# A kernel of four attentions and four feed-forward layers: the softmax maximum of the narrow attentions carried in spare rows of the score product

## The reference

```python
q = (layernorm(x) @ Wq).reshape(B, S, 32, 16)
k = (ctx @ Wk).reshape(B, S, 8, 16)          # repeated for 4 query heads each
v = (ctx @ Wv).reshape(B, S, 8, 16)
scores = einsum('bhqd,bhkd->bhqk', q, k) / 4
probs = softmax(scores, axis=-1)
x = x + einsum('bhqk,bhkd->bhqd', probs, v).reshape(B, S, 512) @ Wo
```

## Time and profile before

| | |
|---|---|
| median of 3 runs | 2164.53 us (2162.89 to 2166.49) |
| profiled execution, first to last instruction | 2159.1 us |
| PE busy in it | 1995.0 us, 92% |
| DVE, ACT, POOL busy | 1587.5, 1335.2, 204.8 us |

### The profile page before, as it was taken

The page is one execution under the profiler, slowest core; times in us unless marked ns, Lnnn a source line. Parts: engine busy times, 40 slices in busy tenths (PEclk is TensorE's granted clock), DMA queues, the critical chain, the costliest instruction groups (busy, mean ns, idle before and its releaser), DMA issues.

```text
span 2159.1 us, 39910 instructions
## 1 busy us (share of the span) xinstructions
PE 1995.0 (92%) x13920; PEld 1147.6 (53%) x13920; DVE 1587.5 (74%) x4091; ACT 1335.2 (62%) x3897; POOL 204.8 (9%) x207
## 2 busy tenths in 40 slices
PE   4887999999999999999976797999999999999778
PEld 2554444466666666666643464444555555555444
DVE  6666555677777777777768576767798889988773
ACT  3665212287777777777753565434788888888621
POOL 3674000000000000000000463000000000000020
PEclk8899999999999999999998998999999999999999
DMA  5231111224444544453530331111044333343200
GB/s 215 62 55 16 59 59 40 78 58 95 108 81 91 110 85 91 81 114 74 95 79 20 74 69 36 59 69 49 16 93 92 71 90 93 62 90 83 62 6 39
DMA packets 318935, 157.65 MB, mean 73 GB/s; under 512 B 309648, under 2 KB 309648, under 8 KB 311312
## 3 DMA queue, kind: packets, MB, share of 16 engines
q1 hardware_dynamic: 318736, 155.09, 31.2%
HBM read 77.44 MB, written 2.10 MB: 37 GB/s over the span
## 4 chain that ended last, share of the span: by engine, by line
PE 59%; DVE 26%; ACT 8%; issue 4%; DMA 1%; POOL 1%; SPq 0%; ACTq 0%; DVEq 0%; POOLq 0%
PE bank L702 54%; ACT hid L1628 4%; DVE hid L2221 3%; DVE masked L2180 3%; DVE negmax L2184 2%; DVE wa_lo L1746 2%; DVE x L2193 2%; DVE oT_lo L2211 2%; DVE negmax_n L1920 1%; DVE wo_lo L1746 1%; ACT bd_hi L1505 1%; PE bank L794 1%; PE bank L810 1%; PE bank L811 1%; DVE xnT_lo L1813 1%
## 5 line engine op out<-in xcount | busy, mean ns | idle before, releaser
L702 PE MATMUL bank<-xnT_hi,wa_hi 128*128 128x512 f16 x736 | 279.1, 379 | 4.2 <-PE bank L702 1.8
L702 PE MATMUL bank<-xnT_hi,wa_lo 128*128 128x512 f16 x736 | 279.1, 379 | 0.0
L702 PE MATMUL bank<-xnT_lo,wa_hi 128*128 128x512 f16 x736 | 279.1, 379 | 0.0
L702 PE MATMUL bank<-wo_hi,oT_hi 128*128 128x512 f16 x576 | 221.5, 385 | 28.2 <-DVE oT_lo L2211 27.2
L2221 DVE SCALAR_TENSOR_TENSOR hid<-probs,inv_total,hid 128x256 f16<-128x256 f32 (+1 forms) x512 | 179.9, 413 | 81.4 <-ACT hid L1628 81.4
L702 PE MATMUL bank<-wo_hi,oT_lo 128*128 128x512 f16 x576 | 221.4, 384 | 0.0
L702 PE MATMUL bank<-wo_lo,oT_hi 128*128 128x512 f16 x576 | 221.2, 384 | 0.0
L702 PE MATMUL bank<-wa_hi,xnT_hi 128*128 128x512 f16 (+3 forms) x640 | 203.1, 323 | 6.7 <-DVE hid L1882 2.6
L702 PE MATMUL bank<-wa_lo,xnT_hi 128*128 128x512 f16 (+3 forms) x640 | 203.0, 323 | 0.0
L702 PE MATMUL bank<-wa_hi,xnT_lo 128*128 128x512 f16 (+3 forms) x640 | 202.9, 323 | 0.0
L1587 ACT ACTIVATE probs<-bank,negmax,rms_r 128x256 f32<-128x256 f32 x256 | 140.9, 560 | 96.3 <-DVE negmax L2177 96.3
(11 more groups left out here) (252 smaller groups left out, 4860.3 us busy)
## 6 DMA issues: line engine op xcount, KB each, us to landing
raw<-in_w_qkv_dram SPq DMA_DIRECT2D x18, 1536.0 KB, 7.0
raw<-in_w_out_dram SPq DMA_DIRECT2D x18, 1024.0 KB, 5.3
raw<-in_w_ffn_dram SPq DMA_DIRECT2D x15, 1024.0 KB, 4.9
pT<-hid SPq DMA_TRANSPOSE x256, 3.1
raw<-in_w_ffn0d_dram SPq DMA_DIRECT2D x7, 512.0 KB, 3.5
x<-in_x_dram SPq DMA_DIRECT2D x4, 512.0 KB, 5.5
expert_b<-in_expert_b_dram SPq DMA_DIRECT2D x1, 2048.0 KB, 9.4
kT<-k SPq DMA_TRANSPOSE x128, 2.4
```

Of the source, the lines that this page charges most:

```text
L702: mm = pe.matmul(dst, l, r, start=start and k == 0, stop=stop and k == n - 1)
```

## The change

The negated maximum no longer has a matmul of its own. The keys' fourth slot of 32 rows, which was zero, holds the constant 64, and the fourth slot of the queries holds, for `turned_scores`, the high and low f16 halves of the negated maximum divided by 64. The score product itself then adds it. For `scores` of the same batch, which runs before, the queries' fourth slot is still zero.

- `max_hi` on ACT is now two instructions: the f16 high part of `negmax_n / 64`, and a f32 copy of `negmax_n / 64` (`max_scaled`), from which POOL's `max_lo` subtracts.
- `max_parts` grows from 128 to 512 columns f16, and `turn_max` makes eight transposes in place of one: four column blocks, into bank S0 and once more into bank Q.
- `spread_max` writes rows 96 to 127 of `qst`, heads 0 and 1 by DVE from S0, heads 2 and 3 by ACT from Q, two instructions of 32 x 512 elements each, in place of one DVE instruction of 128 x 512. On ACT it stands in step 7 between `soft` and `v_part`. PE's `turned_scores` of step 0 and the next `scores` wait for both.
- `turned_scores` is one matmul. The constants `chunk_rows`, `max_chunk` and the bf16 identity go; POOL fills the keys' fourth slot with 64 at the start of each narrow attention.
- The slots of `q_parts` and `k_parts` are in another order; their instructions are the same in number and size.

```diff
-        max_rows = bd_flat[:, 2048:3072].bitcast(BF16).rearrange("p (a b) -> p a b", a=2)
+        max_rows = qst[96:128, :, :].rearrange("p a (c h t) -> p a h c t", c=4, h=HPG)
...
-            def ones():
+            def ones(n):
...
-                pool.memset(k_parts[:, :], 0.0).then_inc(nb_kzero, 1)
+                pool.memset(k_parts[:, :], 0.0).then_inc(k_zero, 1)
+                pool.wait_ge(k_zero, n + 1)
+                for m in range(2):
+                    op = pool.memset(k_part_slots[:, 3, m], MAX_SCALE)
+                op.then_inc(nb_kzero, 1)
...
-                pool.tensor_tensor(max_slots[:, 1], negmax_n[:, :].rearrange("p (m h) -> p m h", m=2), max_slots[:, 0],
-                                   ALU.subtract).then_inc(nb_max_lo, 1)
+                src = max_scaled[:, :].rearrange("p (m c h) -> p m c h", m=2, c=4)
+                pool.tensor_tensor(max_slots[:, 1], src, max_slots[:, 0], ALU.subtract).then_inc(nb_max_lo, 1)
...
             pool.tensor_copy(ident_16[:, :], ident)
-            pool.tensor_copy(ident_b[:, :], ident)
-            pool.tensor_copy(chunk_rows[:, :, :], c("max_chunk").unsqueeze(2).broadcast_to([P, G, P]))
...
                         if b:
                             pe.wait_ge(nb_max_rows, BB)
+                            pe.wait_ge(nb_max_rows_act, BB)
...
                 def turn_max(b):
                     pe.wait_ge(nb_max_lo, n * B + b + 1)
-                    pe.transpose(bank[S0][:, :].bitcast(BF16)[:, 0:P], max_parts[:, :], ident_b[:, :]).then_inc(nb_maxT, 1)
+                    if b == 0:
+                        pe.wait_ge(nb_rope_q if n == 0 else nb_qlo, 2)
+                    for to in (S0, Q):
+                        for ch in range(4):
+                            mm = pe.transpose(halves16(to)[:, ch * P:(ch + 1) * P], max_parts[:, ch * P:(ch + 1) * P],
+                                              ident_16[:, :])
+                    mm.then_inc(nb_maxT, 1)
...
                         pe.wait_ge(nb_max_rows, n * B + b + 1)
+                        pe.wait_ge(nb_max_rows_act, n * B + b + 1)
...
-                    to = bank[PT0 + j % 2][:, :]
-                    pe.matmul(to, kst[:, b % 2, ch, m, :], qst[:, b % 2, ch * 512:(ch + 1) * 512], start=True, stop=False)
-                    pe.matmul(to, chunk_rows[:, g, :], max_rows[:, b % 2, :], start=False, stop=True).then_inc(ng_turned, 1)
+                    pe.matmul(bank[PT0 + j % 2][:, :], kst[:, b % 2, ch, m, :], qst[:, b % 2, ch * 512:(ch + 1) * 512],
+                              start=True, stop=True).then_inc(ng_turned, 1)
...
                         act.wait_ge(nb_maxT, BB)
-                    src = negmax_n[:, :].rearrange("p (m h) -> p m h", m=2)
-                    act.activation(max_slots[:, 0], src, ACT.Copy).then_inc(nb_max_hi, 1)
+                        act.wait_ge(nb_max_lo, BB)
+                    src = negmax_n[:, :].rearrange("p (m c h) -> p m c h", m=2, c=4)
+                    act.activation(max_slots[:, 0], src, ACT.Copy, scale=1 / MAX_SCALE)
+                    act.activation(max_scaled[:, :], negmax_n[:, :], ACT.Copy, scale=1 / MAX_SCALE).then_inc(nb_max_hi, 1)
+
+                def spread_max(b):
+                    act.wait_ge(nb_maxT, n * B + b + 1)
+                    src = halves16(Q)[96:128, 0:512].rearrange("p (c t) -> p c t", c=4)
+                    for h in (2, 3):
+                        op = act.activation(max_rows[:, b % 2, h], src, ACT.Copy, scale=c("max_head")[96:128, h:h + 1])
+                    op.then_inc(nb_max_rows_act, 1)
...
                         soft(j)
+                    if g == 7 and f < B:
+                        spread_max(f)
                     if g == 7 and p < B:
                         v_part(p)
                         k_part(p)
...
                     if g == 0 and BB:
-                        dve.wait_ge(nb_max_lo, BB)
+                        dve.wait_ge(nb_max_hi, BB)
...
                     dve.wait_ge(nb_maxT, BB + 1)
-                    if b >= 2:
-                        dve.wait_ge(ng_turned, (BB - 1) * G)
-                    dve.tensor_tensor(max_rows[:, b % 2, :].rearrange("p (h t) -> p h t", h=HPG),
-                                      bank[S0][:, :].bitcast(BF16)[:, 0:P].unsqueeze(1).broadcast_to([P, HPG, P]),
-                                      c("max_head").unsqueeze(2).broadcast_to([P, HPG, P]), ALU.mult).then_inc(nb_max_rows, 1)
+                    src = halves16(S0)[96:128, 0:512].rearrange("p (c t) -> p c t", c=4)
+                    for h in (0, 1):
+                        op = dve.tensor_scalar(max_rows[:, b % 2, h], src, c("max_head")[96:128, h:h + 1], None, ALU.mult)
+                    op.then_inc(nb_max_rows, 1)
```

More of the change, by code:

```diff
@@ L43 @@
 WOUT = HPG * D
+MAX_SCALE = 64.0
 NORM_EPS = 1e-5
@@ L54 @@
 _at = 0
-for _name, _n in (("ident", P), ("max_head", HPG), ("max_chunk", G), ("iota", 16), ("gate_s", FC), ("up_s", FC),
+for _name, _n in (("ident", P), ("max_head", HPG), ("iota", 16), ("gate_s", FC), ("up_s", FC),
                   ("down_s", D), ("q1", 1), ("k1", 1), ("q3", 1), ("k3", 1), ("router1_b", 8),
@@ L293, in build @@
         inv_total_n = sb("inv_total_n", [2, 16], F32)
-        negmax_n = sb("negmax_n", [32], F32)
+        negmax_n, max_scaled = sb("negmax_n", [32], F32), sb("max_scaled", [32], F32)
         hid = sb("hid", [2, D], F32)
         hid_flat = hid[:, :, :].rearrange("p a b -> p (a b)")
[L297 to L301, removed]
+        ident_16 = sb("ident_16", [P], F16)
+        max_parts = sb("max_parts", [4 * P], F16)
+        max_slots = max_parts[:, :].rearrange("p (c s m j h t) -> p s j t m c h", s=4, m=2, j=2, h=HPG, t=2)[:, 3, 0]
         qst = bd_hi
@@ L326, in build @@
         k_parts = squares[:, 0:512].bitcast(F16)
-        q_part_slots = q_parts.rearrange("p (c m s d) -> p s m c d", m=2, s=4, d=ND)
-        k_part_slots = k_parts.rearrange("p (c u s d) -> p s u c d", u=4, s=4, d=ND)[:, :, 0:4:3]
+        q_part_slots = q_parts.rearrange("p (c s m d) -> p s m c d", m=2, s=4, d=ND)
+        k_part_slots = bass.AP(k_parts.tensor, k_parts.offset,
+                               [list(k_parts.ap[0]), [2 * ND, 4], [P + ND, 2], [2 * P, 4], [1, ND]])
         def v_heads(t):
@@ L472, in build @@
                              "nb_max_rows", "nb_inv", "nb_on", "nb_olo", "nb_y", "ng_max"))
+        nb_max_rows_act, k_zero = sem("nb_max_rows_act"), sem("k_zero")
         n_consts, nb_qn, nb_kn, nb_qparts, nb_kparts, ng_plo = (
@@ L671, in _ @@
             pool.tensor_copy(ident_16[:, :], ident)
-            pool.tensor_copy(ident_b[:, :], ident)
-            pool.tensor_copy(chunk_rows[:, :, :], c("max_chunk").unsqueeze(2).broadcast_to([P, G, P]))
             pool.memset(max_parts[:, :], 0.0)
-            ones()
+            ones(0)
             ctx_low(0)
@@ L685, in _ @@
             pool.wait_ge(w_y, UNITS)
-            ones()
+            ones(1)
             zeros(1)
@@ L2533, in lay_out @@
     cols = {
-        "ident": np.eye(P), "max_head": (row % 64 < 32) & (row // 2 % HPG == np.arange(HPG)),
-        "max_chunk": (row % 64 < 32) & (row // 64 * 4 + row % 64 // 8 == np.arange(G)), "iota": np.broadcast_to(np.arange(16), (P, 16)),
+        "ident": np.eye(P), "max_head": (row >= 96) & (row % 16 < 8) & (row // 2 % HPG == np.arange(HPG)), "iota": np.broadcast_to(np.arange(16), (P, 16)),
         "gate_s": a["L0_ffn_gate_s"].reshape(FC, P).T, "up_s": a["L0_ffn_up_s"].reshape(FC, P).T,
```

## The result

The change makes the kernel slower. In five runs of each the median went from 2163.95 us to 2175.7 us (2175.08 to 2181.86); the ratio is 1.0055 [1.0043, 1.0068], some 11.8 us. The forecast of 2164.8 us, no change, with a range up to 2171, was wrong. Of the five runs after, three took 2175.1 to 2175.7 us and two, the profiled one among them, 2180 to 2182 at a lower granted clock (0.966 against 0.968 to 0.970), so the traces of this kernel, e8's too, show some 4 us more than the median lost.

What follows compares the result with a forecast made beforehand. The prediction took PE, DVE and the keys' way to alternate as bound, the keys' DMA setting when scores start. First attention -1.5 us and second +1.8 gave +0.3: 2164.8 us, no change; range 2158.5 to 2171.

Steps and rivals of the forecast that it cites:

- both as a rival: In the narrow attentions, keys' DMA takes over everywhere: issued 0.6 and 1.15 us later, +5.4 us, 2169.9 us; chance 0.12.
- the clock in the weight stretches: While DVE splits weights, PE idles and falls to half clock: two such stretches and longer first wait, +4.8 us; chance 0.10.
- The matmul removed: turned_scores loses its second matmul: 0.65 us at steps 0 to 2, 0.1 at 3 to 5; 0.97 us a batch.
- The transposes: On PE between max_lo and the output projection's second half: seven more at 0.055 us each, 0.39 us a batch.
- The spread: At the hand-over: DVE's pair 0.7 to 1.3 us, ACT's about 1.09; PE's step 0 0.16 to 0.24 us later.
- The keys' DMA: Behind ACT's spread, issued 0.4 and 0.95 us later; with 3.1 us landings, scores start 0.2 and 0.1 us earlier.
- First hand-overs: First two batches of each attention, without output projection as cover: first attention -0.6 us, second +1.4 us.
- PE's busy time: Over the whole kernel, PE's busy time should fall by about 22 us: 28.2 us of matmuls less the added transposes.
- The profiled execution: Profiled span, 2159.1 us, lies 5.4 us under the median; taken as a part outside first and last instruction, unchanged.
- Costed at nothing: ACT's second copy of the maxima ends during POOL's low part; uncovered it would be 0.24 us a batch, 3.8 us.

Runs made afterwards that it cites:

- e8: The changed kernel again, unedited, for a second profiled execution: 2180.55 us (span 2178.8).
- e1: The kernel before without the second matmul of turned_scores alone; the maximum is still found, transposed and spread: 2157.11 us, ratio 0.9965.
- e7: The changed kernel with a second matmul in turned_scores again, one that adds zeros: 2176.66 us, ratio 1.0049 against the kernel before.
- e9: The kernel before again, unedited, for a second profiled execution: 2166.81 us (span 2164.9).
- e5: The kernel before with seven more transposes of the same tile in turn_max, results unused: 2168.64 us, ratio 1.0020.
- e6: The kernel before with ACT's two spread instructions ahead of v_part, results unused, and PE's step 0 waiting for them: 2169.40 us, ratio 1.0026.
- e2: The changed kernel with v_part and k_part ahead of spread_max on ACT: 2170.91 us, ratio 1.0040 against the kernel before.
- e4: The changed kernel with four transposes, DVE alone spreading one column block of all heads at a time, each step awaiting its block: 2158.86 us.

## Why the prediction was wrong

Its mechanism was right in the main. It named the keys' DMA as what sets the scores, ACT's spread as what delays it, and both as a rival; it named the clock in the weight stretches as another. What failed was the sizes: the keys' issue was put too early, PE's clock stood at nothing in the sum, and the two rivals were taken as alternatives. Here both happened, 11.1 us in the attentions where they were given +5.4 and +4.8.

- *The matmul removed.* The 0.1 us for steps 3 to 5 was, if anything, too much: the stretch took 5.81 us before and 5.80 after. Steps 6 and 7 went as said: `max_lo` and the transposes come 0.21 us earlier. The 0.97 us a batch on PE's path is there in e1 where nothing else is late; in the kernel after the time stays when the whole matmul is put back (e7), in part because the clock comes back with it.
- *The transposes.* 0.39 us for seven was measured (0.62 against 0.23). The term of the sum was right and its place wrong: they stand ahead of ACT's spread, so they delay the keys by as much as PE.
- *The spread.* DVE's pair took 0.90 us, within its bounds. ACT's took 1.25, near the upper bound of 1.3; 1.09 was taken, from the exponentials, though the row with a scale for each partition was the nearer one. PE's step 0 is 0.44 us later (2.01 less 1.36, less 0.21), not 0.16 to 0.24.
- *The keys' DMA: the first term that broke the sum.* Against the transposes its issue was put 0.61 and 1.17 us later (0.4 and 0.95 on the clock of the old timeline, plus the 0.22 that the transposes come earlier). Measured were 1.10 and 1.51. Some of the gap is that pair (0.16 and 0.18 us). The rest is `v_part` and `k_part`: in the first attention ACT's `k_part` ends 0.85 us behind the spread where 0.55 was reckoned. The 0.55 came from a stretch in which `v_part` began 0.12 us before the exponential ahead of it had ended, and `k_part` 0.13 us before `v_part` had; now each begins 0.03 us behind the end of the one before. The landing of 3.1 us was right, and so was its reason: the queries' and the keys' DMA are issued 4.0 us apart, 2.7 and 2.3 before. With the measured issue the sum of a steady batch comes out: 1.10 - 0.21 = 0.89 us later on the clock, less the 0.4 that the keys had to spare, is the +0.5 of the first attention; 1.51 - 0.21 = 1.30 less 0.8 to 1.1 is +0.2 to +0.5 in the second, where +0.43 and +0.45 were measured. The prediction had -0.3 and -0.2. It gives the other batches too: with the distances of e9, 4.18 and 4.88 us from the issue to the scores where the landing was long, nothing is lost in the 4th interval of the first attention and 0.3 us won in the 5th of the second (+0.08 and -0.30 measured).
- *First hand-overs.* Predicted -0.6 and +1.4 us, measured +2.7 and +3.0. In the first attention step 0 comes 1.0 us later, as said (2.50 against 1.45 and 2.01 against 1.02), but nothing is won back. In the first of the first attention the scores start hardly later (7.63 us against 7.50, e8 and e9); what came was a fall of the clock in the stretch behind them, 1.25 us for the twelve matmuls; in the second of it a fall took 0.84. The first of the second attention was about right, 1.2 predicted and 1.48 measured. The second of it had 0.2 and took 1.55, of which 1.0 is eighteen matmuls at the half clock.
- *PE's clock: the second term.* The rival's mechanism was right and its places too few: it was priced for two stretches of the second attention and given 0.10, and the sum had nothing for it. The trace after has four falls in places that were full, two of them in the first attention. An estimate of the two terms from these rows: 0.49 and 0.34 us more of issue in five steady batches each are 4.2 us, the four falls 4.3.
- *PE's busy time.* 22 us less was predicted. In the attentions it fell by 7.1 us against e9: matmuls at the half clock count twice. The windows show the lower clock; how much of the missing 15 us is the clock's and how much is that of records of longer matmuls behind a wait is not settled.
- *The profiled execution.* The 5.4 us between the span and the median were taken as a part outside the instructions. Each run's time is only 1.8 us above its span (2180.1 and 2178.3); the rest was one execution that ran faster than the others. It didn't touch the sum.
- *Costed at nothing.* ACT's second copy held: in the hand-over above it ends at 110.16 us, and POOL's `max_lo` starts at 111.11, behind its low part.

The parts don't add up. Taken singly they are -7.8 (e1), +3.7 (e5) and +4.5 us (e6), together +0.4; the kernel after has +11.8. e1 and e7 point to the reason: the saving of 7.8 us holds only while the keys are on time. With ACT's pair in front of them it is gone, and the transposes, which stand in front of the pair, come on top: 3.7 + 4.5 = 8.2 us. The 3.6 that are left are of the size of the four falls of the clock, 4.3 us. Both steps are argued: no run adds the parts one by one, and e7 lost three of the falls and got the time back elsewhere. What e6, e2 and e4 show is that ACT's pair makes the keys late, that they are on time again once the pair is out of their way, and that a kernel with neither wait is faster than the one before.

What stays open: the last batch of the second attention, 2.07 us longer up to its transposes and 1.2 shorter behind them, where the chain runs over POOL; and why the second hand-over there, 16.7 us in the kernel before, takes 18.3 to 21.6 in all kernels but e4 (16.24), e1 (19.04) among them, in which no key is late.

## What to carry to other kernels

When PE's work is cut in a loop where a transfer arrives just behind it, the saving is capped by the distance between the two, and any step put on the transfer's way is charged in full: measure that distance first (here 0.4 us in one attention and 0.8 to 1.1 in the other). A helper that spreads data for the next step should be cut so that the first user waits for its own piece only, and queued behind whatever feeds a DMA; e4 differs from the kernel after in that, and in four transposes, and is 17 us faster. Read the granted clock stretch by stretch as well: the four intervals with a fall of it are 7.6 of the 12.4 us that all 14 lost in the traces. Price an edit with all its parts in place, since savings that are not on the path any more don't pay for the parts that are.

## What the runs showed of the hardware

Seven more transposes of 128 columns of 16 bit cost 0.39 us back to back, 0.055 each.

ACT took 671 ns for a copy of 32x512 from PSUM with a scale for each partition, out of 16-bit as out of f32 PSUM (1.25 us for two in e6 as well); DVE took 0.90 us for two of the same, and 0.70 us for one `TENSOR_TENSOR` of the same size.

A weight split on DVE takes up to two and a half times as long beside POOL (0.68 us alone, 1.67 at 80.99 us of the kernel before). Timelines of DVE and POOL, first of the kernel after, then of the kernel before, at the same place:

```profile
1267.11 1.57 DVE L1768 SCALAR_TENSOR_TENSOR wa_lo<-raw,wa_hi 128x512 f16<-128x512 f32 x1
...
1266.96 1.16 POOL L651 TENSOR_TENSOR qT_lo<-probs,qT_hi 128x512 f16<-128x512 f32 x1 [1.49 <-ACT qT_hi L1447]
...
1257.08 0.68 DVE L1746 SCALAR_TENSOR_TENSOR wa_lo<-raw,wa_hi 128x512 f16<-128x512 f32 x1
...
1257.42 2.65 POOL L645 TENSOR_TENSOR qT_lo<-probs,qT_hi 128x512 f16<-128x512 f32 x2 [1.50 <-ACT qT_hi L1427]
```

After, POOL's low part is running when the split begins and goes on beside it for 1.01 us: 1.57 us. Before, it began when half of the split was done: 0.68, as much as the splits at 1324.79 and 1327.82 us took with nothing on POOL. So what counted here was which of the two began first. That is 0.9 of the 3.3 us of this interval, through an order that the change never touched: the scores came later, and POOL's work didn't.
